# Graph attention after a linear-attention block: queries and keys projected right behind the first half of the block, with a reordered high/low tile and one row DMA

## What is computed

```
x = x + gated_linear_attention_block(layernorm(x))       # 4 heads, chunks of 64, then a gated MLP of 352
x = x + graph_ffn(layernorm(x))

graph_ffn: nodes[-1] = input; for c in 0..5 (three earlier nodes feed each):
    q = ew[c,0] * (nodes[c-1]   @ We[eq] + be[eq])
    k = ew[c,1] * (nodes[first] @ We[ek] + be[ek])
    v = ew[c,2] * (nodes[mid]   @ We[ev] + be[ev])
    nodes[c] = act_w[c] * (softmax((q@Wq)(k@Wk)^T / sqrt(16)) (v@Wv)) @ Wo[c] + q      # 8 heads of 16
output = layernorm(nodes[5]) * ln_g + ln_b
```

## Time and profile before

| what | value |
|---|---|
| median of three runs | 1070.54 us |
| the profiled execution | 1071.46 us, span 1069.7 us |
| TensorE busy | 995.8 us (93%) |
| VectorE / ScalarE / GpSimd busy | 837.9 / 730.5 / 447.4 us |
| packets of SyncE's DMA queue | 82974, 51.7% of the 16 DMA engines' time |
| chain that ended last | TensorE 48%, DMA 17% (all of it `mst<-mrows`), VectorE 12%, SyncE's queue 9% |
| granted TensorE clock, mean | 0.983 of full speed |

### The profile page before, as it was taken

One profiled execution on the slowest core, in us unless ns is written; L12 is line 12 of the kernel. 1 busy time (PEld: TensorE's weight loads), 2 busy tenths in 40 slices (PEclk: granted clock), 3 DMA queues, 4 the chain that ended last, 5 costly groups with the idle time before them and its releaser, 6 DMA issues.

```text
span 1069.7 us, 26895 instructions
## 1 busy us (share of the span) xinstructions
PE 995.8 (93%) x9705; PEld 704.7 (66%) x9705; DVE 837.9 (78%) x1805; ACT 730.5 (68%) x1601; POOL 447.4 (42%) x874
## 2 busy tenths in 40 slices
PE   8989999998899999999999999999999999999995
PEld 4755655655566776776767777767666766776663
DVE  5466777766689988887887899888788878878895
ACT  3345666664577777777777778877777777777775
POOL 3522232233333343334444358843433344443365
PEclk9889999999899999999999999999999999999998
DMA  8100000006476667667676776677676667766651
GB/s 226 34 1 1 1 0 0 0 2 89 70 104 97 95 92 107 101 97 103 96 105 93 105 104 109 115 112 102 91 106 101 98 100 103 100 92 105 102 75 33
DMA packets 84695, 87.33 MB, mean 82 GB/s; under 512 B 11642, under 2 KB 70526, under 8 KB 84574
## 3 DMA queue, kind: packets, MB, share of 16 engines
q1 hardware_dynamic: 82974, 83.69, 51.7%
q0 software_dynamic: 800, 1.98, 0.9%
q10 hardware_dynamic: 800, 0.05, 0.0%
HBM read 6.90 MB, written 2.10 MB: 8 GB/s over the span
## 4 chain that ended last, share of the span: by engine, by line
PE 48%; DMA 17%; DVE 12%; SPq 9%; issue 5%; ACT 5%; POOL 3%; DVEq 0%; POOLq 0%; ACTq 0%
PE bank L1289 46%; DMA mst<-mrows 17%; SPq L502 6%; DVE region L1155 3%; SPq L516 2%; POOL hl L592 2%; ACT region L817 1%; DVE region L1087 1%; DVE region L971 1%; DVE region L1082 1%; PE bank L1625 1%; ACT region L793 1%; DVE region L1075 1%; DVE region L1036 1%; POOL hl L589 0%
## 5 line engine op out<-in xcount | busy, mean ns | idle before, releaser
L1155 DVE TENSOR_REDUCE region<-bank 128x2 f32<-128x512 f32 x768 | 488.9, 680 | 124.5 <-PE bank L1289 118.5
L817 ACT ACTIVATE region<-bank 128x512 f32<-128x512 f32 x768 | 409.7, 609 | 60.6 <-PE bank L1289 60.6
L1289 PE MATMUL bank<-st 48*128 48x256 f32 x3072 | 325.0, 330 | 5.6 <-DVE region L1155 4.2
L1289 PEld LDWEIGHTS bank<-st 48*128 48x128 f32 x3072 | 250.7, 189 | 28.0 <-DVE region L1155 4.7
L589 POOL TENSOR_TENSOR hl<-qk,one_col 128x512 fp32r<-128x512 f32 x96 | 100.1, 1043 | 400.1 <-ACT qk L782 400.1
L1289 PE MATMUL bank<-region 128*32 128x256 f32 (+3 forms) x3554 | 250.0, 377 | 2.2 <-DVE region L1182 1.2
L1289 PEld LDWEIGHTS bank<-region 128*32 128x32 f32 (+2 forms) x3554 | 130.9, 117 | 85.4 <-issue 16.6
L1289 PE MATMUL bank<-mst,ones 64*128 64x512 bf16 x768 | 151.3, 387 | 27.5 <-DMA mst<-mrows 25.1
L592 POOL TENSOR_TENSOR hl<-qk,hl 128x512 fp32r<-128x512 f32 x96 | 122.6, 1277 | 7.5
L839 ACT ACTIVATE mrows<-bank 24x256 bf16<-24x256 bf16 x96 | 35.8, 373 | 126.6 <-PE bank L1625 126.6
L1289 PEld LDWEIGHTS bank<-mst,ones 64*128 64x128 bf16 x768 | 37.2, 93 | 91.4 <-DMA mst<-mrows 40.4
(11 more groups left out here) (193 smaller groups left out, 1276.3 us busy)
## 6 DMA issues: line engine op xcount, KB each, us to landing
st<-hl SPq DMA_DIRECT2D x576, 128.0 KB, 4.5
mst<-mrows SPq DMA_DIRECT2D x192, 6.0 KB
out<-xall POOLq DMA_DIRECT2D x14, 128.0 KB, 3.8
xall<-in_L_attn_hidden_states SPq DMA_DIRECT2D x1, 768.0 KB, 8.4
cst<-in_constants SPq DMA_DIRECT2D x1, 514.5 KB, 4.1
xT<-in_L_ffn_Wq SPq DMA_DIRECT2D x1, 384.0 KB
xT<-in_L_ffn_Wk SPq DMA_DIRECT2D x1, 384.0 KB
xT<-in_L_ffn_Wv SPq DMA_DIRECT2D x1, 384.0 KB
```

The source lines that it names most:

```text
L817: act.activation(to, x_bank(x, k, e)[:, :].rearrange("p (j q) -> p j q", j=2), ACT.Exp).then_inc(B["exp_ok"], 1)
L1155: dve.tensor_reduce(mx[s.n % 2][:, to:to + 2], s_bank(s, k, e)[:, :].rearrange("p (j k) -> p j k", j=2), AX_X, ALU.max, negate=True).then_ ...
L1289: return pe.matmul(o, w, x, start=start, stop=stop, skip_group_check=skip)
```

## The change

1. TensorE: `pv(d)` is cut into its two halves (16 products each). The transposes of the maxima stand between them, and `project_qk(a)` directly behind the second half. `project(d)` is cut in two as well: its `w_res` product (`residual`) goes to where `project_qk` was, the `w_out` product stays at the end of the slot.
2. ScalarE: `copy_qk(a)` goes from behind `exps(x,2)` to behind `copy_rows(m)`, ahead of `exps(x,1)`.
3. The parts in `hl` stand as K high, Q low, K low, Q high, so two of three pairs lie side by side instead of one. GpSimd's two instructions address them with other steps; of SyncE's six stack DMAs four go in 2048-byte pieces where two did.
4. SyncE brings `mrows` to `mst` in one DMA of six partitions, 24 apart, and its semaphore counts 16 a step, not 32.

```diff
-K_HI, K_LO, Q_HI, Q_LO = range(4)
+K_HI, Q_LO, K_LO, Q_HI = range(4)
...
-                for s in range(2):
-                    of = s * MROW * JH
-                    sp.dma_start(mst[m.n % 2][HALF * s:HALF * s + MROW, :, :], mrows[m.n % 2][of:of + MROW * JH, :]).then_inc(m_in[m.n % 2], 16)
+                sp.dma_start(mst[m.n % 2][0:(2 * MROW - 1) * MSTEP + 1:MSTEP, :, :], mrows[m.n % 2][:, :]).then_inc(m_in[m.n % 2], 16)
...
                 if m is not None:
                     copy_rows(m)
+                if a is not None:
+                    copy_qk(a)
                 if x is not None:
                     exps(x, 1)
...
                     exps(x, 2)
-                if a is not None:
-                    copy_qk(a)
...
                 if d is not None:
-                    pv(d)
+                    pv_ready(d)
+                    pv_half(d, 0)
...
                     transpose_maxima(m)
+                if d is not None:
+                    pv_half(d, 1)
+                if a is not None:
+                    project_qk(a)
                 burst((1, 2), (2,))
...
-                if a is not None:
-                    project_qk(a)
+                if d is not None:
+                    residual(d)
                 burst((3,), (3,))
```

More of the change, by code:

```diff
@@ L51 @@
 MCOLS = 2 * MROW * JH
+MSTEP = 24
 UNITS = 8
@@ L588, in split @@
                 pool.wait_ge(B["qk_ok"], a.n + 1)
-                pool.tensor_tensor(to[:, 0::2, :], qk[a.n % 2], one_col[:, :].unsqueeze(2).to_broadcast([P, 2, T]), ALU.mult)\
+                pool.tensor_tensor(to[:, K_HI::Q_HI - K_HI, :], qk[a.n % 2], one_col[:, :].unsqueeze(2).to_broadcast([P, 2, T]), ALU.mult)\
                     .then_inc(B["hi_ok"], 1)
                 pool.wait_ge(B["hi_ok"], a.n + 1)
-                pool.tensor_tensor(to[:, 1::2, :], qk[a.n % 2], to[:, 0::2, :].bitcast(F32), ALU.subtract)\
+                pool.tensor_tensor(to[:, K_LO:Q_LO - 1:-1, :], qk[a.n % 2], to[:, K_HI::Q_HI - K_HI, :].bitcast(F32), ALU.subtract)\
                     .then_inc(B["lo_ok"], 1)
@@ L837, in copy_rows @@
                 if old is not None:
-                    act.wait_ge(m_in[old.n % 2], 32 * old.uses(2))
+                    act.wait_ge(m_in[old.n % 2], 16 * old.uses(2))
                 act.activation(mrows[m.n % 2][:, :], bank[IN][0:MCOLS, 0:P].bitcast(BF16), ACT.Copy).then_inc(B["mt_ok"], 1)
@@ L1602, in weights @@
                 if k == 0:
-                    pe.wait_ge(m_in[x.n % 2], 32 * x.uses(2))
+                    pe.wait_ge(m_in[x.n % 2], 16 * x.uses(2))
                 for e in range(2):
@@ L1626, in transpose_maxima, with pv_ready @@
                 k.then_inc(B["mt_ps"], 1)
-            def pv(d):
+            def pv_ready(d):
                 pe.wait_ge(B["exp_ok"], d.n * UNITS + UNITS)
@@ L1637, in pv, with pv_half, residual @@
                         pe.wait_ge(B["node_ok"], old.nodes())
[L1638 to L1646, removed]
+            def pv_half(d, g):
+                for kt in range(KT):
+                    for j in range(GCOL):
+                        h = g * GCOL + j
+                        k = mm(bank[OUT][32 * j:32 * j + 32, g * T:(g + 1) * T], vaug[d.n % VALS][:, kt, VW * h:VW * h + VW],
+                               probT[d.n % 2][:, kt * H + h, :], start=(kt == 0), stop=(kt == KT - 1), skip=True)
+                if g == 1:
+                    k.then_inc(B["pv_ok"], 1)
+            def residual(d):
                 to, prev = bank[OUT], source(d, GRAPH[d.c]["src"][0])
@@ L1650, in project @@
                     mm(to[:, T:2 * T], w_res[:, d.c, :], prev, stop=False)
-                    pe.wait_ge(B["ctxT_ok"].sem, B["ctxT_ok"].at(d.n))
+                else:
+                    for t in range(KT):
+                        mm(to[:, T + t * P:T + (t + 1) * P], prev[:, t * P:(t + 1) * P], w_res[:, d.c, :], start=(t == 0), stop=False, skip=True)
+            def project(d):
+                to = bank[OUT]
+                pe.wait_ge(B["ctxT_ok"].sem, B["ctxT_ok"].at(d.n))
+                if not d.last:
                     mm(to[:, T:2 * T], w_out[:, d.c, :], ctxT, start=False).then_inc(B["node_ps"].sem, 1)
                 else:
-                    pe.wait_ge(B["ctxT_ok"].sem, B["ctxT_ok"].at(d.n))
                     for t in range(KT):
-                        r, o = slice(t * P, (t + 1) * P), slice(T + t * P, T + (t + 1) * P)
-                        mm(to[:, o], prev[:, r], w_res[:, d.c, :], stop=False)
-                        k = mm(to[:, o], ctxT[:, r], w_out[:, d.c, :], start=False)
+                        k = mm(to[:, T + t * P:T + (t + 1) * P], ctxT[:, t * P:(t + 1) * P], w_out[:, d.c, :], start=False, skip=True)
                     k.then_inc(B["node_ps"].sem, 1)
```

## The result

| | before | after |
|---|---|---|
| median | 1069.72 us (4 runs, 1068.23 to 1070.84) | 1108.29 us (4 runs, 1106.02 to 1109.21) |
| profiled execution | 1071.46 us | 1106.02 us |

The ratio is 1.0379, 95% interval 1.0357 to 1.0401: the change costs 3.8%.

A forecast was written before the change was run, and what follows sets the result against it. TensorE was taken to pace the graph stage, with a DMA wait and a hidden ScalarE limit. Its terms made the slot 8.55 us against 8.17, over 92 slots +35 us on 1071.46, forecast 1105 us; range 1084 to 1123.

The forecast's parts named there:

- the stretch: TensorE from the first matmul of weights(x,1) to the block behind scores(s,3), w_res inside: forecast at 3.48 us.
- the slot's beginning: TensorE's weights(x,0) with scores 0 and 1 at the start of each slot: 1.03 us.
- second entry: TensorE's second half of the value products, beginning behind the transposes: taken as 0.05 us, bounds 0 and 0.11.
- the projection: TensorE's projection of Q and K, losing its 0.11 us entry behind the value products: 0.96 us instead of 1.07.
- the rival of a second wait: project_qk on TensorE also waits for copy_rows: at 0.2 us a slot, +18 us, 1123 us; chance 0.08.
- ScalarE paces the stretch: From weights(x,1) to scores(s,3) ScalarE's exponentials, 0.48 us apart, set the time; TensorE's projection only filled it.
- The DMA wait goes: TensorE's wait for mrows to mst ahead of weights(x,0) vanishes: alone 0.38 us a slot, 35 us in all.
- three reasons: For the row DMA's wait ending: transposes half the value products earlier, one issue replacing two, earlier copy_qk freeing SyncE.
- The rest costs nothing: Stacks, new order in hl and GpSimd's instructions, even doubled (1.04 us more), cost 0 us in the loop.
- The copies hide: ScalarE's start is set by weights(x,1) alone: slot 8.32 to 8.4 us, 1085 to 1092 us; chance 0.14.
- The clock falls: TensorE's granted clock drops to 0.96, its own list grows by 4%: +18 us, 1123 us; chance 0.06.
- ScalarE keeps up: ScalarE does not hold scores(s,3), TensorE runs its own list: slot 7.84 us, -30 us, 1040 us; chance 0.09.

The follow-up runs named there:

- e1: The changed kernel with only ScalarE's list undone, the copies of Q and K again between exps(x,2) and exps(x,3): 1175.48 us, ratio 1.0992.
- f1: The changed kernel with project_v moved from the slot's end to behind w_res, ahead of weights 3 and scores 3: 1092.05 us, ratio 1.0212.
- f2: The changed kernel with the w_res product put back right ahead of w_out: 1148.12 us, ratio 1.0733.
- e4: The changed kernel with the two row DMAs of before in place of one: 1109.52 us, ratio 1.0364.
- e7: The kernel before with only the single row DMA and the new order of the parts in hl: 1066.66 us, ratio 0.9972.
- f4: e7 with the transposes behind three quarters of the value products instead of behind all: 1070.99 us, ratio 1.0006.
- e2: The changed kernel with project_qk, w_res and the copies of Q and K back in their old places: 1077.3 and 1083.1 us in two usable runs.
- e5: e1 with GpSimd's split of the maxima between high and low Q and K, and SyncE's row DMA between high and low stacks: 1188.28 us.

## Why the prediction was right, and where it was not

**The sum.** Forecast 1105 us, measured 1108.29. The new slot was forecast at 8.55 and is 8.59. Term by term: the stretch 3.48, measured 3.46; `w_out` 0.54 and 0.54; the values 0.54 and 0.54; the slot's beginning 1.03 and 1.03; value products and transposes with their second entry 2.00, measured 609.90 - 607.95 = 1.95; the projection 0.96, measured 1.07. That last one is the mis-sized term: I had its entry vanish behind the value products, and it stayed. The mean is 8.61 and not 8.59 because a few slots are longer. Four between 330 and 401 us take 8.92 or 9.18 (356.38 to 365.56, below); they also carry the last tiles of the first stage, which the prediction did not mention. Seven with a finished element take 8.74 to 8.81 (8.81 between the projections of two of them, 653.07 and 661.88), as the rival of a second wait had it.

```profile
356.38 0.39 PE L1288 MATMUL bank<-mst,ones 64*128 64x512 bf16 x2
...
365.56 0.39 PE L1288 MATMUL bank<-mst,ones 64*128 64x512 bf16 x2
...
653.07 1.10 PE L1288 MATMUL bank<-xT,w_fold 128*128 128x256 f32 x4
...
661.88 1.10 PE L1288 MATMUL bank<-xT,w_fold 128*128 128x256 f32 x4 [0.16 <-issue]
```

**ScalarE paces the stretch.** Shown, by e1 (3.31 with late copies, 3.46 with early ones), and by f1 and f2 (3.46 and 3.48 with 0.54 more and 0.43 less work in it). The row it came from was the slot without a projection. The six exponentials in a row take 3.03 us, again 0.48 apart.

**The DMA wait goes.** Right in what happens and in when the row DMA is issued: forecast 2.66 us into the slot, measured 609.59 - 606.92 = 2.67. I had given three reasons, and they do not weigh alike. One issue instead of two is neither needed (e4 has two issues and no wait) nor enough (e7 has one and the wait). Transposes half the value products earlier are not enough (f4 has early ones and the wait). The third, the early `copy_qk`, is what clears SyncE's queue for the early issue: its stack DMAs are through at 604.58 + 3.81 = 608.39 in the changed kernel, 1.2 us ahead of the row DMA at 609.59, where in the rows of e7 and f4 above the row DMA goes out less than 0.3 us behind them.

```profile
604.58 3.81 SPq L503 DMA_DIRECT2D st<-hl  x6
```

But a rival to all three stands: the slot itself is longer now. In the kernel before the rows are there 611.63 - 603.72 = 7.91 us into their slot, in e7 620.78 + 4.65 - 617.07 = 8.36, and both would be in time for a slot of 8.59. e1 shows it. Its row DMA goes out directly behind the stacks too, yet its TensorE waits only 0.8 us for `mst` in the whole span; the next slot, at 604.38, begins without a wait:

```profile
595.47 5.29 SPq L503 DMA_DIRECT2D st<-hl  x6
600.86 0.77 SPq L515 DMA_DIRECT2D mst<-mrows  x1
```

No run has the early copies in a slot of about 7.8 us, so it is not shown that they would end the wait there. By an estimate from the rows they would: 2.67 and the longest landing of e7, 4.85, make 7.52.

The page DMA: Bandwidth & Descriptors of the Trainium skill, section Queues, rings and completion order, says that each DMA engine consumes one queue's descriptors in ring order. The landing that hardly moved with one issue less, in e7, fits that, and would fit a fixed time of the transfer as well; the two were not measured apart.

**"The rest costs nothing".** Right for the change and wrong as I gave it. I wrote that even doubled GpSimd instructions would cost nothing, and that the stacks have the whole slot as cover. e1 and e2 show GpSimd's order on the path as soon as its input is late, and e5 shows a wait of over 1 us for the stacks. In the changed kernel neither holds TensorE up: the split of the maxima (L610, 607.36) waits for VectorE and no longer for the split of Q and K, and the stacks are not among TensorE's waits.

**The rivals.** The copies hide: refuted by e1, 0.15 us a slot. The clock falls: it did not, 1.00 from 300 to 1000 us:

```profile
300.00:1000.00 700.00, 662.67 (x7024) 467.73 (x7024) 555.03 (x1047) 496.77 (x1087) 299.29 (x591) 1.00 0.66 96
```

ScalarE keeps up: refuted by the slot itself.

**What stays open.** e2's number rests on two runs. Which of the early copies and the longer slot took the DMA wait away was not separated. Whether an order exists that has the early copies and enough filler was tried only in f1, which VectorE's maxima then limit; f1 is still 2.1% slower than the kernel before.

## What to carry to other kernels

A block of matmuls between two waits on another engine can be free filler: take the time of that stretch in a place where the block is missing, and if it is as long there, moving the block out costs its full length elsewhere. Before an engine's wait is put down to the transfer that ends it, look at what the issuing queue did just before. A buffer that nobody waits for has a slack in microseconds; write it down, because the next reordering spends it.

## What the runs showed of the hardware that I had not expected

A block of fp32 passes pays its entry although other fp32 passes stand right ahead of it. The projection takes 1.07 us in the earlier trace rows, behind a burst on `st`, and 1.07 us (610.97 - 609.90) behind value products, where I had taken 0.11 off. In a slot where the timeline lists its two products apart (333.26, 333.80, next burst 334.33), the first takes 0.54, as `w_res` does where it begins a block. The value products ahead of it have 32 columns each, the projection 128; which difference keeps the entry was not tried. And the extra switch between value products and transposes, for which I had set up to 0.11, showed no cost: both together take 1.95 us in the earlier trace rows and 1.95 with it.
